# The same operations in another order: stage slots of a four-engine pipeline on a grid of a sixteenth of a recurrence step

## The reference, cut to what matters

```python
xn = layernorm(x)                                  # x: 4 x 4096 x 512
# branch s: a recurrence over every second position
x_sub = rmsnorm(xn[:, ::2]) * g_norm
x_proj, gate = split(x_sub @ w_in.T + b_in)
def step(h, xt):                                   # h: 4 x 512 x 64
    h = tanh(h * A + xt[:, :, None] * Bm)
    return h, h @ c_sum + Dv * xt
h_last, ys = scan(step, 0, x_proj)                 # 2048 steps, one after another
s = repeat(ys * silu(gate) @ w_out.T + b_out, 2)
# branch g: a mixture of experts on each token
spikes = sigmoid(xn @ W_enc + b_enc)               # 512 -> 1024
cont = spikes @ W_s2c + b_s2c                      # 1024 -> 64
gates = normalised top 2 of softmax(cont @ Wr + br) over 8 experts
expert_out = sum over experts of gates * (relu(cont @ W1 + b1) @ W2 + b2)
spikes2 = sigmoid(expert_out @ W_c2s + b_c2s)      # 64 -> 1024
g = silu(layernorm(spikes2 @ W_dec + b_dec) * ln_g + ln_b)
out = x + s * g
```

## Time and profile before

| | us |
|---|---|
| median of 3 runs | 6132.56 |
| lowest and highest run | 6130.13, 6157.22 |
| profiled execution | 6143.14 |
| its span | 6141.3 |
| PE busy | 5782.2 (94%) |
| DVE busy | 5633.2 (92%) |
| POOL busy | 5300.8 (86%) |
| ACT busy | 4209.2 (69%) |

### The profile page before, as it was taken

How to read it: one execution, slowest core, us unless ns; L and a number is a source line. 1 busy time by engine, 2 the same in 40 slices (tenths; PEclk the granted TensorE clock), 3 DMA queues, 4 the chain that set the end, 5 groups by cost and what they waited for, 6 DMA issues and landing times.

```text
span 6141.3 us, 87284 instructions
## 1 busy us (share of the span) xinstructions
PE 5782.2 (94%) x28640; PEld 3187.1 (52%) x28640; DVE 5633.2 (92%) x9556; ACT 4209.2 (69%) x8981; POOL 5300.8 (86%) x2828
## 2 busy tenths in 40 slices
PE   5999999999999999999999999999999999999998
PEld 3555555555555555555555555555555555555554
DVE  4999999999999989999999999999999999999997
ACT  3677676676776767667767667677676676676775
POOL 3888888888888878888888888888888988888887
PEclk9999999999999989999999999999999999999999
DMA  5444444444444444444444444444444444444443
GB/s 143 109 109 107 114 105 110 117 99 114 113 108 114 106 100 112 105 114 109 107 114 105 110 117 99 114 111 107 115 106 109 114 104 111 114 102 114 112 107 86
DMA packets 158073, 673.34 MB, mean 110 GB/s; under 512 B 45619, under 2 KB 46643, under 8 KB 92083
## 3 DMA queue, kind: packets, MB, share of 16 engines
q1 hardware_dynamic: 151488, 658.29, 44.5%
q10 hardware_dynamic: 6132, 9.47, 0.6%
HBM read 617.25 MB, written 50.33 MB: 109 GB/s over the span
## 4 chain that ended last, share of the span: by engine, by line
PE 39%; DVE 31%; ACT 18%; issue 11%; ACTq 1%; POOL 0%; DVEq 0%; DMA 0%; SPq 0%; POOLq 0%
DVE ps_z L1033 15%; PE bank L877 13%; ACT h L554 12%; DVE ps_z L1027 11%; PE ps_y L789 6%; PE ps_acc L889 5%; PE bank L809 4%; PE bank L950 4%; PE ps_acc L837 2%; ACT wide L582 2%; PE bank L863 2%; DVE g L1098 1%; DVE g L1113 1%; DVE conte L1107 1%; ACT squares L661 1%
## 5 line engine op out<-in xcount | busy, mean ns | idle before, releaser
L480 POOL TENSOR_TENSOR u<-xb,bt 128x1024 f32<-128x1024 f32 x2048 | 4811.0, 2361 | 469.1 <-DVE ps_z L1033 432.4
L554 ACT ACTIVATE h<-ps_z 128x512 f32<-128x512 f32 x4096 | 2418.0, 600 | 1375.6 <-DVE ps_z L1033 1358.0
L1027 DVE TENSOR_TENSOR ps_z<-h,ps_A 128x512 f32<-128x512 f32 x4096 | 2689.1, 692 | 376.0 <-ACT h L554 277.4
L1033 DVE TENSOR_TENSOR ps_z<-ps_z,u 128x512 f32<-128x512 f32 x4096 | 2666.4, 691 | 0.6 <-POOL u L480 0.6
L877 PE MATMUL bank<-wide,w 65*128 65x256 f32 x4096 | 1021.6, 393 | 0.4
L789 PE MATMUL ps_y<-h,c_wide 128*32 128x512 f32 x8192 | 987.1, 600 | 2.0 <-ACT h L554 2.0
L822 PE MATMUL bank<-xnT,w_enc 128*128 128x256 f32 x4096 | 911.4, 381 | 0.0
L877 PEld LDWEIGHTS bank<-wide,w 65*128 65x128 f32 x4096 | 741.4, 191 | 286.6 <-issue 154.6
L822 PEld LDWEIGHTS bank<-xnT,w_enc 128*128 128x128 f32 x4096 | 774.3, 190 | 181.4 <-issue 83.4
L809 PE MATMUL bank<-w_in,xnT 128*128 128x512 f32 x1024 | 468.4, 601 | 90.6 <-ACT xnT L572 90.6
L789 PEld LDWEIGHTS ps_y<-h,c_wide 128*32 128x32 f32 x8192 | 214.1, 109 | 531.3 <-issue 385.4
(11 more groups left out here) (117 smaller groups left out, 4373.9 us busy)
## 6 DMA issues: line engine op xcount, KB each, us to landing
xb<-x_proj_scratch SPq DMA_DIRECT2D x2048, 256.0 KB, 4.5
xbuf<-in_L_attn_x SPq DMA_DIRECT2D x256, 128.0 KB
xres<-in_L_attn_x SPq DMA_DIRECT2D x512, 64.0 KB
out<-g SPq DMA_DIRECT2D x256, 128.0 KB
x_proj_scratch<-xp SPq DMA_DIRECT2D x256, 64.0 KB
w_enc<-in_L_ffn_W_enc ACTq DMA_DIRECT2D x1, 2048.0 KB
w_dec<-in_L_ffn_W_dec ACTq DMA_DIRECT2D x1, 2048.0 KB
w_in<-in_L_attn_w_in SPq DMA_DIRECT2D x1, 2048.0 KB, 16.8
```

The lines of the kernel that those rows point to most:

```text
L480: pool.tensor_tensor(u[:, tau % 2, :, :], xt, bt[:, :, :], ALU.mult).then_inc(u_ready, 1)
L554: act.activation(h[:, tau % RING, f, :], ps_z[:, f, :], ACT.Tanh).then_inc(h_ready, 1)
L1027: dve.tensor_tensor(ps_z[:, f, :], h[:, (tau - 1) % RING, f, :], ps_A[:, f, :], ALU.mult).then_inc(m_done, 1)
L1033: dve.tensor_tensor(ps_z[:, f, :], ps_z[:, f, :], u[:, tau % 2, f, :], ALU.add).then_inc(z_ready, 1)
```

## The change

The constants of nearly all stages on POOL, ACT, PE and DVE are replaced; SP's stay. `run_bodies` now walks in sixteenths of a step on every engine (`GRAIN = 16`) and issues a part of a step whenever the grid meets it, so a stage can stand at any sixteenth. What stands behind a given part still comes out as: after that part and before the next; the finer numbers order the stages that stand between the same two parts, and, on PE, order all stages. The second `scale_cont` of a block now has the same two waits as the first. Nothing else differs: the same instructions with the same operands.

```diff
@@ -31,6 +31,7 @@
 SP = 32
 F = S // SP
 STEPS = 32
+GRAIN = 16
 QUAD = 4
 NQ = STEPS // QUAD
 CK = 4
@@ -63,51 +64,51 @@
 SP_STORE_SCRATCH = -17
 SP_RESIDUAL = (36, 47)
 SP_STORE_OUT = 55
-POOL_PROJ_SCALE = -25
-POOL_DEC_SCALE = (30, 36)
-POOL_FIN_SKIP = 32
-POOL_FIN_GATE = 37
-POOL_FIN_ADD = (51, 59)
-ACT_PROJ_NORM = -24.5
-ACT_PROJ_EVAC = (-24.5, -23.0)
-ACT_GATE_SILU = -5.5
-ACT_SPIKES = (0.5, 2.5, 3.5, 4.5)
-ACT_CONTT_COPY = 5.5
-ACT_ROUTE_SIG = 8.0
-ACT_SCALE_CONT = (9.5, 10.5)
-ACT_CONTET_COPY = (11.5, 11.5, 12.5, 12.5)
-ACT_GATET_COPY = 14.0
-ACT_RELU = (13.5, 13.5, 14.5, 14.5, 15.5, 15.5, 16.5, 16.5, 17.5, 17.5, 18.5, 19.5, 19.5, 20.5, 21.5, 21.5)
-ACT_EO_COPY = 22.5
-ACT_SPIKES_AGAIN = (23.5, 24.5, 25.5, 25.5)
-ACT_DEC_SILU = (35.5, 39.0)
-ACT_DEC_SQUARE = (29.0, 31.5)
-ACT_PROJ_MOMENTS = -25.5
-ACT_FIN_EVAC = 38
-ACT_OUT_SEED = 37
-ACT_DEC_SEED = (24.5, 25.5)
-PE_Y = (5, 15, 18, 22, 29, 32, 34, 36)
-PE_PROJ_TRANSPOSE = (-23, -22)
-PE_PROJ_IN = (-21, -19)
-PE_ENCODE = (2, 4, 4, 4)
-PE_CONTROLLER = 5
-PE_ROUTER = 8
-PE_CONTET = (15, 15, 16, 16)
-PE_GATET = 18
-PE_EXPERTS = (19, 19, 19, 19, 19, 20, 22, 24, 28)
-PE_TO_SPIKES = (30, 30, 30, 30)
-PE_DECODE = (32, 34)
-PE_FIN_TRANSPOSE = 40
-PE_FIN_OUT = 41
-DVE_PROJ_STATS = -25.5
-DVE_PROJ_EVAC = (-22.0, -20.25)
-DVE_ROUTE = (7.5, 7.75, 8.0, 8.25, 8.25, 8.5)
-DVE_ROUTE_GATE = 9.75
-DVE_DEC_SCALE = (30.75, 36.75)
-DVE_DEC_SHIFT = (32.5, 37.75)
-DVE_FIN_Y = 35.25
-DVE_FIN_MUL = 40.0
-DVE_PROJ_AGGR = -25.5
+POOL_PROJ_SCALE = -23.8125
+POOL_DEC_SCALE = (31.8125, 33.5625)
+POOL_FIN_SKIP = 35.25
+POOL_FIN_GATE = 38.375
+POOL_FIN_ADD = (53.8125, 61.4375)
+ACT_PROJ_NORM = -24.4375
+ACT_PROJ_EVAC = (-23.4375, -23.125)
+ACT_GATE_SILU = -2.25
+ACT_SPIKES = (1.6875, 3.375, 3.5, 5.5)
+ACT_CONTT_COPY = 6.625
+ACT_ROUTE_SIG = 9.25
+ACT_SCALE_CONT = (9.75, 10.6875)
+ACT_CONTET_COPY = (11.6875, 11.6875, 11.6875, 12.6875)
+ACT_GATET_COPY = 13.8125
+ACT_RELU = (13.3125, 13.75, 13.9375, 14.5, 15.75, 15.875, 16.5, 16.5, 18.6875, 18.875, 19.875, 19.9375, 20.6875, 20.875, 21.875, 21.9375)
+ACT_EO_COPY = 22.9375
+ACT_SPIKES_AGAIN = (23.875, 24.8125, 25.5, 26.875)
+ACT_DEC_SILU = (32.5, 36.9375)
+ACT_DEC_SQUARE = (29.625, 31.1875)
+ACT_PROJ_MOMENTS = -25.1875
+ACT_FIN_EVAC = 38.6875
+ACT_OUT_SEED = 38.5625
+ACT_DEC_SEED = (24.875, 26.625)
+PE_Y = (9.375, 10.25, 14.75, 19.375, 21.875, 28.625, 38.9375, 40.125)
+PE_PROJ_TRANSPOSE = (-21.8125, -21.75)
+PE_PROJ_IN = (-21.75, -21.75)
+PE_ENCODE = (8.75, 8.75, 8.8125, 9.1875)
+PE_CONTROLLER = 9.5625
+PE_ROUTER = 10.0
+PE_CONTET = (10.8125, 12.0625, 12.125, 17.5)
+PE_GATET = 17.3125
+PE_EXPERTS = (17.75, 18.25, 18.25, 19.0625, 19.875, 19.875, 20.0625, 21.375, 21.6875)
+PE_TO_SPIKES = (22.3125, 26.25, 27.8125, 27.8125)
+PE_DECODE = (33.5625, 36.5)
+PE_FIN_TRANSPOSE = 41.6875
+PE_FIN_OUT = 42.125
+DVE_PROJ_STATS = -25.0625
+DVE_PROJ_EVAC = (-21.25, -20.125)
+DVE_ROUTE = (7.9375, 8.25, 8.4375, 8.75, 9.3125, 9.5)
+DVE_ROUTE_GATE = 9.9375
+DVE_DEC_SCALE = (31.9375, 33.875)
+DVE_DEC_SHIFT = (32.75, 36.5)
+DVE_FIN_Y = 36.0625
+DVE_FIN_MUL = 40.875
+DVE_PROJ_AGGR = -24.9375
 
 
 def build(nc, x, w_inT, b_in, A_T, B_T, Cm, Dv, w_outT, b_out, g_norm, W_enc, b_enc, W_s2c, b_s2c,
@@ -350,21 +351,20 @@
         def run_bodies(eng, steps, between, parts=1):
 
             def body(blk, par):
-                for n in range(STEPS * parts):
-                    slot = n / parts
-                    steps(blk, slot)
+                for n in range(STEPS * GRAIN):
+                    slot = n / GRAIN
+                    if n % (GRAIN // parts) == 0:
+                        steps(blk, slot)
                     if not is_first(blk):
                         between(blk - 1, 1 - par, slot + STEPS)
                     between(blk, par, slot)
                     if not is_last(blk):
                         between(blk + 1, 1 - par, slot - STEPS)
 
-            body(0, 0)
-            for blk in range(1, LAST):
+            for blk in range(NB):
                 body(blk, blk % 2)
-            body(LAST, LAST % 2)
-            for n in range(STEPS * parts):
-                between(LAST, LAST % 2, STEPS + n / parts)
+            for n in range(STEPS * GRAIN):
+                between(LAST, LAST % 2, STEPS + n / GRAIN)
 
         def is_first(blk):
             return isinstance(blk, int) and blk == 0
@@ -610,10 +610,9 @@
 
             def scale_cont(blk, q):
 
-                if q == 0:
-                    act.wait_ge(gate_ready, blk + 1)
-                    if not is_first(blk):
-                        wait_filled(act, fin_fill(blk - 1, FILL_FIN + 1))
+                act.wait_ge(gate_ready, blk + 1)
+                if not is_first(blk):
+                    wait_filled(act, fin_fill(blk - 1, FILL_FIN + 1))
                 act.activation(conte[:, q, :, M], gate[:, q, :], ACT.Copy)
                 for e in range(E):
                     ins = act.activation(conte[:, q, e, 0:M], cont_acc[:, q, :], ACT.Copy,
```

## The result

The changed kernel takes 5848.65 us (median of 4 runs, 5841.24 to 5854.47) against 6139.79 for the kernel before beside it; the ratio is 0.9522, with a 95% interval of 0.9495 to 0.9549.

The account below looks back on a forecast made before the run. Bound: PE and DVE, both nearly full, waiting for each other. Start-up 105.2, 63 laps of 91.2 (90.5 + 0.7) or 5745.6, tail 99 and 1.8 around the span gave 5952, forecast as 5948 us; range 5890 to 6040.

Parts of the forecast that it names:

- The walk of a lap: One lap of the new order added up stage by stage from row durations; it closes at 90.5 us for PE and DVE.
- PE's waits: PE in the new lap: 0.46 us idle among the experts' inputs and 0.45 for spikes3 before the controller.
- The stalls at relu 0 and relu 15: Relu 0 at step 13 and relu 15 at step 22 come late in the new order, 0.4 us each.
- The term for the burst: ACT's three operations at 25.5 (1.94 us) are spread out, so the 0.56 us they cost goes.
- y1 between the transposes: On PE, y1 (1.85 us) fills the wait for the second bank; of 0.45 + 0.36 + 1.46 only issue gaps stay.
- the clock: TensorE clock dips in 4 laps of 10 at about 1.5 us: 0.6 us a lap, plus 0.1 for small issue gaps.
- rival B: The clock stays up, with 63 laps of 90.5 us, about 5910 us; chance 0.16.
- the 1.33 us in front of the controller: PE's idle there goes because the second half's shift moves from 5.75 to 4.5 on DVE.
- The tail: The last block and its tail go from 102.1 to 99 us; the recurrence saves some 3.
- C: Lateness returns in new places, such as y6 behind both decodes: 1 to 1.5 us a lap, 6010 to 6045; chance 0.20.
- E: Nothing moves: PE idles before y7 with all encoders behind it, 6105 to 6160 us; chance 0.07.
- D: Slower: the long clock fall in the experts becomes common at 17.5 us each; 15 of 64 laps give 6210; chance 0.05.

Follow-up runs that it names:

- pe_less_work: The changed kernel without the second half of the states in y1 and y4, 1.85 us less PE work a lap: 5849.39 us, clean lap 89.41.
- pe_old_order: The changed kernel with only PE's constants put back to those before the change: 6219.42 us, ratio 1.0117, clean lap 93.15.
- controller_waits: The changed kernel with dec_shift of the second half at 6.5 instead of 4.5 and its dec_silu at 6.9: 5918.38 us, clean lap 90.50.
- dve_old_places: The changed kernel with only DVE's constants put back to those before the change: 6448.89 us, ratio 1.0492.
- walker_old_order: The changed code (walk in sixteenths, two more waits) with all constants of the kernel before: 6146.81 us, ratio 1.0005, clean lap 93.40.
- shift_back_alone: The changed kernel with dec_shift of the second half back at 5.75 and its dec_silu at 5.9: 5853.48 us, clean lap 89.42.
- y3_sooner: The changed kernel with y3 behind experts 2 instead of experts 3: 5924.35 us, ratio 0.9637, clean lap 90.47.
- pe_new_order_alone: All constants of the kernel before, but PE's of the changed kernel: 6242.82 us, ratio 1.0156, clean lap 95.40.
- all_together: The changed kernel with two more covered DVE operations, y2 directly ahead of the experts and y3 behind experts 2: 5922.61 us, clean lap 90.41.
- y2_before_experts: The changed kernel with y2 moved behind the gate's and last input's transposes, directly ahead of the experts: 5854.74 us, clean lap 89.66.

## Why the prediction was right or wrong

**Right: the mechanism.** Two nearly full engines waited for each other through ACT's program order, and the new order took most of the waits out. The walk of a lap came close at every station, and always a little late. It had DVE reach step 7 again 0.3 us before the controller's end, and so it is (3068.48, controller's end 3068.8). DVE's step 9 starts 6.9 us after step 7 (7.1 in the walk), step 12 15.9 (16.3), step 15 24.0 (24.5), the next step 0 68.4 (69.0), the next step 7 89.4 (90.2). PE's waits were forecast as 0.46 in the experts' inputs and 0.45 at the controller, for spikes3; they are 0.62 and 0.50. The stalls at relu 0 and relu 15 were forecast as 0.4 each and are 0.28 and 0.45. The term for the burst (0.56) measured 0.52. y1 between the transposes, for which the walk had no figure of its own, is worth 1.20.

**Wrong: the lap of the walk, 90.5 us where 89.43 were measured (67 us in all).** This is the term that failed, and both of its sides were too long. On PE I added up stages with about the durations that their rows show. Such a duration holds the end of the last matmul too, and the next stage starts before it. From start to start the stages are shorter: both projections 6.87 us instead of 2 x 3.62, fin_out 3.54 instead of 3.70, a decode 6.96 instead of 7.06, an encoder 3.50 instead of 3.54. By the end of the projections the walk was already 1.0 us late on PE. On DVE, the side that bounds the lap (pe_less_work), the walk had 81.9 for the steps, 7.1 for the work between them and 1.2 of stalls, 90.2 in all; the step distances give 81.9, 6.7 and 0.8. The work was smaller by 0.3 at the route, the aggregate and fin_mul and by 0.1 at the statistics, and of the stalls only the two at the relus came. The last 0.3 of the 90.5 the walk took from PE, which came round later than DVE; but PE does not bound the lap.

The same mistake stands behind the range: I called PE's 89.16 us of work a floor that a lap of 90.2 hardly passes. It is 88.06 for the same instructions. That fits the rows: a stop on PE shows the end of the stage before it as busy time, which a next stage otherwise covers by some 0.16 us (fin_out, 3.70 long, has the next stage 3.54 behind its start). How the 1.10 divide over the stops is not shown.

**Wrong: the clock (44 us charged, 12.6 paid).** I charged 0.6 us a lap for dips and 0.1 for gaps left out. There is not one dip near the controller in 63 laps, only two long falls. The rival B (chance 0.16), in which the clock stays up, had no dips either, but it took 63 laps of the same 90.5 us and came to about 5910. I had kept the dips because the same small matmuls stand there. Their 0.6 us a lap was my estimate, 4 laps of 10 at 1.5 us with PE as the bound; no row shows that price, and PE is not the bound (pe_less_work). The dip in the second lap of the earlier trace rows, 3.4 us with the granted clock at 0.50, cost 94.35 - 93.42 = 0.93 us, and the 33 before the change 0.93 to 1.47, 1.05 in the mean; in pe_old_order one in the second place cost 1.58 (94.73 - 93.15). The small matmuls are still there and bring no dip. Nor is the gap in front of the controller enough: it is 1.33 us before the change, with 33 dips, and 1.28 us in controller_waits, with none; in dve_old_places it is 2.24 us, and 30 of 63 laps have a dip. What brings them stays open. And walker_old_order shows that dips in every second lap weren't a property of the old order, as I had read them from one execution.

**Wrong: one step with the right outcome.** Of the 1.33 us in front of the controller only the forecast 0.5 is left, but that is not the shift's doing (shift_back_alone: 0.0). The controller now comes later in DVE's steps, 1.4 us into step 6 instead of 0.2, when the shift is done at either place. For this step the outcome was luck.

**Small terms.** The tail took 93.8 us, not 99: y7 starts 71.7 us behind the last controller instead of 78.1, and the last fin_out found the clock up (3.70 us, where it took 5.26 before). The start took 4.2 more, where I had nothing; why, no run shows. Together: 67.4 + 44.1 - 12.6 + 5.2 - 4.2 = 99.9, the distance from the sum of the terms, 5951.6, to the profiled 5851.7.

**The rivals.** C (new lateness) and E (nothing moves) did not come; their mechanisms are real and lie close, as y3_sooner (+1.04), controller_waits (+1.07) and pe_new_order_alone (+2.0 a lap) show. D was right in kind, long falls where it put them, but not in number or price. Its 17.5 us stands in no row, and was too high already for the old order: the lap with the fall took 106.48 us where a clean one takes 93.42, so 13.06. The range was too narrow below, since all of its cases were built on the same durations.

## What to carry to other kernels

When several engines are over 90% busy, walk one lap with start-to-start distances from stretches in which the stages follow each other, not with the durations of single rows; a busy time in which stops occur is not a floor (89.16 us of PE work in a lap before, 88.06 after, for the same instructions). Change the places of stages on all engines together: half of a good order can be worse than the old one. And look at the length of every lap, not only at the time: here it repeats within 0.02 us and separates what a place costs from what the clock costs, as in pe_old_order, where the two have opposite signs.

## What the runs showed of the hardware that I had not expected

In the changed kernel the granted clock of TensorE fell from 1.00 to 0.50 in two of 63 laps, each time 8 us after PE's last gap. In all the long falls of these runs it stayed at 0.50 for 10 to 27 us among the experts' matmuls, with PE busy; it rose while y3 ran, or, in y3_sooner and all_together, up to 0.6 us before y4. The same order of instructions had 33 dips and one long fall in one execution (before), and 8 and four in another (walker_old_order). In one comparison the executions of the kernel before spread over 80 us (6107.89 to 6188.25), those of y2_before_experts beside them, whose profile has no fall, over 8 (5852.80 to 5860.78).
